# x and eps written into zeroed PSUM by ScalarE and VectorE instead of by identity matmuls, with x loaded one image of each half at a time

## The reference

```
x = x + L0(gn(x))    # contextual attention
x = x + L1(gn(x))    # 3x3 convolution, 64 to 64 channels, plus bias
```

## Time and profile before

| | us |
|---|---|
| median of 3 runs (lowest, highest) | 35.08 (35.05, 35.92) |
| the profiled execution | 34.43 |
| its span, first to last instruction | 32.5 |

### The profile page before, as it was taken

How to read it: one execution, slowest core, us unless ns; L and a number is a source line. 1 busy time by engine, 2 the same in 40 slices (tenths; PEclk the granted TensorE clock), 3 DMA queues, 4 the chain that set the end, 5 groups by cost and what they waited for, 6 DMA issues and landing times.

```text
span 32.5 us, 1877 instructions
## 1 busy us (share of the span) xinstructions
PE 26.9 (83%) x820; PEld 20.3 (62%) x820; DVE 17.8 (55%) x70; ACT 14.5 (45%) x41; POOL 12.6 (39%) x37
## 2 busy tenths in 40 slices
PE   0699999999969978995999799979999999991000
PEld 0314515317919957973998889749996999970000
DVE  0068280698479098459757183784869658005000
ACT  1940000697979992080934507078420890005000
POOL 3999999580676818870000000730028000000000
PEclk9999999999999999999999999999999999999999
DMA  0029679600000000000382000000000000440180
GB/s 0 0 55 303 174 215 365 234 0 0 0 20 0 0 0 0 20 0 10 49 113 35 5 0 0 20 0 0 0 20 0 0 0 20 163 160 0 39 284 0
DMA packets 4215, 1.87 MB, mean 58 GB/s; under 512 B 2800, under 2 KB 4080, under 8 KB 4208
## 3 DMA queue, kind: packets, MB, share of 16 engines
q1 hardware_dynamic: 3344, 1.24, 13.6%
q10 hardware_dynamic: 864, 0.53, 5.6%
HBM read 1.09 MB, written 0.52 MB: 50 GB/s over the span
## 4 chain that ended last, share of the span: by engine, by line
PE 66%; DVE 9%; POOL 9%; issue 5%; ACT 2%; POOLq 0%; DVEq 0%
PE X L508 20%; PE X L414 14%; PE X L486 13%; PE Y L498 4%; PE X L425 3%; PE Y L473 3%; DVE b_sb L672 3%; POOL rnorm L249 2%; ACT e_sb L339 2%; POOL gn_rstd L249 2%; PE X L418 2%; PE X L454 2%; PE X L444 2%; DVE pst L657 2%; DVE o_sb L704 1%
## 5 line engine op out<-in xcount | busy, mean ns | idle before, releaser
L414 PE MATMUL X<-idle 128*128 128x512 f16 x10 | 4.6, 607 | 1.1 <-POOL idle L230 1.1
L249 POOL TENSOR_TENSOR hn_rstd<-hn_mv,neg_half 128x2 f32<-128x2 f32 x2 | 1.4, 688 | 8.7 <-DVE hn_mv L602 8.7
L486 PE MATMUL X<-k_sb,pst 64*64 64x128 f32 (+2 forms) x144 | 4.4, 263 | 0.4 <-DVE pst L657 0.4
L508 PE MATMUL X<-x2h,whl 64*64 64x256 f16 x144 | 4.7, 274 | 0.0
L486 PEld LDWEIGHTS X<-k_sb,pst 64*64 64x64 f32 x144 | 3.9, 133 | 0.7 <-issue 0.5
L508 PEld LDWEIGHTS X<-x2h,whl 64*64 64x64 f16 x144 | 4.1, 106 | 0.0
L436 PE MATMUL X<-fst 64*64 64x64 f32 x144 | 2.7, 222 | 0.3 <-DVE fst L612 0.3
L414 PEld LDWEIGHTS X<-idle 128*128 128x128 f16 x10 | 1.0, 127 | 3.0 <-issue 1.9
L436 PEld LDWEIGHTS X<-fst 64*64 64x64 f32 x144 | 2.4, 134 | 0.7 <-DVE fst L612 0.7
L473 PE MATMUL Y<-xh,pair_k 64*64 64x256 f32 x16 | 2.8, 444 | 0.0
L508 PE MATMUL X<-x2l,whl 64*64 64x256 f16 x72 | 2.4, 274 | 0.0
(11 more groups left out here) (83 smaller groups left out, 56.9 us busy)
## 6 DMA issues: line engine op xcount, KB each, us to landing
k_sb<-k_dram SPq DMA_DIRECT2D x1, 288.0 KB, 3.6
xh<-x_in_dram SPq DMA_DIRECT2D x2, 128.0 KB, 3.0
xh<-x_in_dram ACTq DMA_DIRECT2D x2, 128.0 KB, 3.6
out_dram<-o_sb ACTq DMA_DIRECT2D x2, 128.0 KB, 2.1
out_dram<-o_sb SPq DMA_DIRECT2D x2, 128.0 KB, 2.1
k_sb<-c_dram SPq DMA_DIRECT2D x1, 192.0 KB, 3.3
whl<-whl SPq DMA_DIRECT2D x2, 72.0 KB, 3.1
w_sb<-weight_in_dram SPq DMA_DIRECT2D x1, 72.0 KB, 3.6
```

The source lines that it names most:

```text
L249: return pool.tensor_tensor(dst, src, neg_half[:, 0:dst.shape[1]], ALU.pow)
L414: te.matmul(fill_ps, idle[:, 0:P], idle[:, :], start=True, stop=True)
L486: i = te.matmul(b_ps[u][half(o ^ h), h, q0:q0 + step * (nq - 1) + 1:step, :], pst[u][half(o), 1 - t, h, G * (1 - s):G * (1 - s) + L], sh, ...
L508: i = te.matmul(conv_ps[u][half(t), h, :], whl[half(h), w, k, :], xp[u][half(h), t, k // 3:k // 3 + H, k % 3:k % 3 + W], start=False, stop ...
```

## The change

- x: the eight identity matmuls of `put_x` on PE are replaced by four ScalarE copies from SBUF to PSUM. For that each of the eight banks is first written once with zeros by one of the 512-column matmuls (`fill`), counted in `bank_set`; later matmuls in those banks add (`start=False`).
- eps: `add_eps` (eight matmuls before the first statistics, four at the end of each `deconv`) goes; VectorE writes eps into the zeroed banks after the third fill. `hn_ps[1]` moves from column 448 to 472. The fills in front of the first `pair_statistics` go from eight to seven; behind it one (the eighth bank) is added, and one more stands before `gram(0, 0)`.
- x loads: each is one image of each half, on 128 partitions, with a semaphore of its own, and the statistics of image t wait for load t alone. The output goes with it: a store now holds both images of one half (64 partitions), and waits for both ScalarE's and VectorE's result.
- zeroing: POOL zeroes only the borders of f, y, y1 and p, and the fp16 tensors as fp32 words; VectorE no longer zeroes f.
- lists: on PE the mask product goes between parts 0 and 1 of `gram(1)`, `transpose_f(1)` goes ahead of `fuse2(1)`, and `deconv(0)` has one shift of unit 1 ahead of it and three behind it, before the second statistics. On DVE `keep_mask` (now with a memset of `mask_ps` behind it) goes ahead of `normalise_gram(0)`, both `gated_weight` behind `largest(0)`, `copy_ft(1)` ahead of the wait for `deconv(0)`. On ACT the four `put_x` stand first, and `exp_logits(0)` ahead of `high_weight`.

```diff
-        fill_ps = X[0][:, 0, :]
-
-        xh_in = unit_sems("xh_in")
+        banks = [X[1][:, 1, :], X[1][:, 0, :], X[0][:, 0, :], Y[0][:, 0, :], Y[0][:, 1, :], Y[1][:, 0, :],
+                 X[0][:, 1, :], Y[1][:, 1, :]]
+
+        xh_in = [[sem(f"xh_in{u}{t}") for t in t2] for u in u2]
...
-        xhv = x.rearrange("(u h t) c s -> u h c t s", u=UNITS, h=2)
-        ov = out.rearrange("(u h t) c s -> u h (t c) s", u=UNITS, h=2)
...
+        xhv = x.rearrange("(u t h) c s -> u t (h c) s", u=UNITS, t=IPU)
+        ov = out.rearrange("(u t h) c s -> u t c h s", u=UNITS, t=IPU)
...
-            sp.dma_start(xh[0][half(0), :, :], xhv[0, 0]).then_inc(xh_in[0], 16)
-            sp.dma_start(xh[1][half(0), :, :], xhv[1, 0]).then_inc(xh_in[1], 16)
+            for u in u2:
+                sp.dma_start(xh[u][:, 0, :], xhv[u, 0]).then_inc(xh_in[u][0], 16)
...
-                sp.wait_ge(out_ready[u], 1)
-                sp.dma_start(ov[u, 1], o_sb[u][:, 1, :]).then_inc(stored, 16)
+                sp.wait_ge(out_ready[u], 2)
+                sp.dma_start(ov[u, 1], o_sb[u][half(1), :, :]).then_inc(stored, 16)
...
-            link(pool.memset(eps_sb[:, :, :], 0.0))
-            pool.memset(eps_sb[:, :, 2], GN_EPS * 2 * HW).then_inc(small_set, 1)
-            for u in u2:
-                pool.memset(y[u][:, :, :], 0.0).then_inc(att_zero, 1)
-                pool.memset(y1[u][:, :, :], 0.0).then_inc(att_zero, 1)
-            for u in u2:
-                pool.memset(pst[u][:], 0.0).then_inc(att_zero, 1)
-            for u in u2:
-                pool.memset(x2h[u][:, :, :, :], 0.0).then_inc(x2_zero, 1)
-                pool.memset(x2l[u][:, :, :, :], 0.0).then_inc(x2_zero, 1)
-            pool.wait_ge(small_set, 2)
+            for u in u2:
+                pool.memset(pads(fst[u][:]), 0.0).then_inc(f_zero, 1)
+                for edge in edges(fst[u]):
+                    pool.memset(edge, 0.0).then_inc(f_zero, 1)
+            for u in u2:
+                pool.memset(y[u][:, :, 0:PADL:PADL - 1], 0.0).then_inc(att_zero, 1)
+                pool.memset(y1[u][:, :, 0:PADL:PADL - 1], 0.0).then_inc(att_zero, 1)
+            for u in u2:
+                pool.memset(pads(pst[u][:]), 0.0).then_inc(att_zero, 1)
+                for edge in edges(pst[u]):
+                    pool.memset(edge, 0.0).then_inc(att_zero, 1)
+            for u in u2:
+                pool.memset(x2h[u][:, :, :, :].bitcast(fp32), 0.0).then_inc(x2_zero, 1)
+                pool.memset(x2l[u][:, :, :, :].bitcast(fp32), 0.0).then_inc(x2_zero, 1)
+            pool.wait_ge(small_set, 1)
...
-            act.dma_start(xh[0][half(1), :, :], xhv[0, 1]).then_inc(xh_in[0], 16)
-            act.dma_start(xh[1][half(1), :, :], xhv[1, 1]).then_inc(xh_in[1], 16)
+            for u in u2:
+                act.dma_start(xh[u][:, 1, :], xhv[u, 1]).then_inc(xh_in[u][1], 16)
...
+            def put_x(u, t):
+                act.wait_ge(bank_set, 1 + (3, 4, 5, 7)[2 * u + t])
+                act.wait_ge(xh_in[u][t], 16)
+                act.activation(x1_ps[u][:, t, :], xh[u][:, t, :], ACT.Copy).then_inc(x_put[u], 1)
...
-                act.activation(o_sb[u][:, 0, :], conv_ps[u][:, 0, :], ACT.Identity, bias=bias, scale=1.0 / W_SCALE).then_inc(act_step, 1)
-                act.wait_ge(act_step, u + 1)
-                act.dma_start(ov[u, 0], o_sb[u][:, 0, :]).then_inc(stored, 16)
...
+                act.activation(o_sb[u][:, 0, :], conv_ps[u][:, 0, :], ACT.Identity, bias=bias, scale=1.0 / W_SCALE
+                               ).then_inc(out_ready[u], 1)
+                act.wait_ge(out_ready[u], 2)
+                act.dma_start(ov[u, 0], o_sb[u][half(0), :, :]).then_inc(stored, 16)
...
+            for u in u2:
+                for t in t2:
+                    put_x(u, t)
             weight_scales()
...
+            exp_logits(0)
             high_weight()
-            exp_logits(0)
-            act.wait_ge(att_zero, 6)
+            act.wait_ge(att_zero, 10)
             left_of_p(0)
             copy_ft(0)
...
+            def fill(ps):
+                return te.matmul(ps, idle[:, 0:P], idle[:, :], start=True, stop=True)
+
             def keep_clock(n):
                 for _ in range(n):
-                    te.matmul(fill_ps, idle[:, 0:P], idle[:, :], start=True, stop=True)
-
-            def add_eps(ps):
-                for h in h2:
-                    te.matmul(ps[half(h), :, :], eye(h), eps_sb[half(h), :, :],
-                              start=True, stop=False, skip_group_check=True)
+                    fill(banks[6])
...
-                            i = te.matmul(gram_ps[u][half(t), h, :], f, f, start=n == di == 0, stop=n == 2 and di == 2)
+                            i = te.matmul(gram_ps[u][half(t), h, :], f, f, start=False, stop=n == 2 and di == 2,
+                                          skip_group_check=True)
...
-                te.wait_ge(x_put[u], 4)
+                if u:
+                    te.wait_ge(mask_gone, 1)
...
-            def put_x(u, t):
-                te.wait_ge(xh_in[u], 32)
-                for h in h2:
-                    te.matmul(x1_ps[u][half(h), t, :], eye(h), xh[u][half(h), t, :],
-                              start=True, stop=False, skip_group_check=True).then_inc(x_put[u], 1)
...
             def deconv(u):
                 te.wait_ge(ft_ready[u], 2)
                 te.wait_ge(b_ready[u], 2)
+                te.wait_ge(x_put[u], 2)
                 for q in range(4):
                     for h in h2:
                         for t in t2:
@@ -498,7 +513,6 @@
                             i = te.matmul(px[:, q // 2, q % 2], ft[u][half(t ^ h), h, q, :],
                                           b_sb[u][half(t ^ h), h, q, :], start=False, stop=True, skip_group_check=True)
                 i.then_inc(dec_done[u], 1)
-                add_eps(hn_ps[u])
...
             te.wait_ge(idle_set, 1)
-            keep_clock(4)
+            for ps in banks[0:7]:
+                fill(ps).then_inc(bank_set, 1)
             te.wait_ge(pair_k_set, 2)
-            te.wait_ge(small_set, 2)
-            add_eps(gn_ps[0])
-            add_eps(gn_ps[1])
-            keep_clock(4)
+            te.wait_ge(gn_eps, 1)
             pair_statistics(gn[0], gn_ps[0])
-            put_x(0, 0)
+            fill(banks[7]).then_inc(bank_set, 1)
             keep_clock(2)
             pair_statistics(gn[1], gn_ps[1])
+            keep_clock(1)
             gram(0, 0)
             gram(0, 1)
             gram(0, 2).then_inc(gram_done[0], 1)
-            put_x(0, 1)
             gram(1, 0)
+            te.wait_ge(k_late_in, 16)
+            te.wait_ge(mask_cell, 1)
+            te.wait_ge(bank_set, 8)
+            te.matmul(mask_ps, mint[:, :].broadcast_to([L, P]), kb(K_WINDOW)[half(0)], start=False, stop=True,
+                      skip_group_check=True).then_inc(mask_sum, 1)
             gram(1, 1)
             gram(1, 2).then_inc(gram_done[1], 1)
-            te.wait_ge(k_late_in, 16)
-            te.wait_ge(mask_cell, 1)
-            te.matmul(mask_ps, mint[:, :].broadcast_to([L, P]), kb(K_WINDOW)[half(0)], start=True, stop=True
-                      ).then_inc(mask_sum, 1)
             fuse1(0)
             transpose_f(0)
             te.wait_ge(mask_ready, 1)
             fuse2(0)
             fuse1(1)
-            put_x(1, 0)
-            put_x(1, 1)
+            transpose_f(1)
             fuse2(1)
             te.wait_ge(k_shift_in, 16)
             sum_shifts(0, range(9)).then_inc(b_done[0], 1)
-            transpose_f(1)
+            sum_shifts(1, range(0, 1))
             deconv(0)
-            sum_shifts(1, range(0, 3))
+            sum_shifts(1, range(1, 4))
+            te.wait_ge(hn_eps, 2)
             pair_statistics(hn[0], hn_ps[0])
-            sum_shifts(1, range(3, 9)).then_inc(b_done[1], 1)
+            sum_shifts(1, range(4, 9)).then_inc(b_done[1], 1)
             start_from_x1(0)
             deconv(1)
...
-            for u in u2:
-                dve.memset(fst[u][:], 0.0).then_inc(f_zero, 1)
-
-            def statistics(n, src):
+            dve.wait_ge(bank_set, 3)
+            eps_of_gn = X[1][:, :, 448:448 + 4 * STATS].rearrange("p h (t k) -> p h t k", t=2)[:, :, :, 2]
+            dve.memset(eps_of_gn, GN_EPS * 2 * HW).then_inc(gn_eps, 1)
+            for u in u2:
+                dve.memset(hn_ps[u][:, :, 2], GN_EPS * 2 * HW).then_inc(hn_eps, 1)
+
+            def statistics(n, src, landed=None):
                 for t in t2:
+                    if landed:
+                        dve.wait_ge(landed[t], 16)
                     dve.bn_stats(n.stats[:, t, :], src[:, t, :]).then_inc((n.half_stats, n.stats_ready)[t], 1)
...
+                dve.wait_ge(mask_ready, 1)
+                dve.memset(mask_ps, 0.0).then_inc(mask_gone, 1)
...
-            dve.wait_ge(xh_in[0], 32)
-            statistics(gn[0], xh[0])
+            statistics(gn[0], xh[0], xh_in[0])
             moments(gn[0], gn_ps[0])
```

(18 more changed lines are left out.)

21 lines of the change are left out of this document (12 added, 9 removed).

## The result

The changed kernel takes 36.4 us (median of five runs, 35.91 to 36.77) against 35.05 for the kernel before (34.05 to 35.92): a ratio of 1.058, 95% interval 1.039 to 1.076. It is slower. The prediction said 34.55, 34.0 to 35.35, with 6% for slower.

The account below looks back on a forecast made before the run. It took one chain of latencies, not one full engine, as the bound. Profiled 34.43 - 0.55 (convolution start) + 0.07 (stores) = 33.95; the median lies 0.65 above, 34.6; forecast 34.55 us, range 34.0 to 35.35.

Parts of the forecast that it names:

- GpSimd's border memsets replace larger ones; they end no later than before.: Front: GpSimd's zeroing was to end no later than before; no cost to VectorE was counted.
- done by 3.2: Front: VectorE's three eps memsets, behind the third fill at about 2.6, were to be done by 3.2 us.
- The pair statistics start at 4.7.: Front: first pair statistics on TensorE at 4.7 us against 5.28, a gain of 0.6.
- That rival: Front gains more: first load lands well before 4.0, everything before y(0) moves by -0.9; 34.0 to 34.3 us, chance 0.25.
- The clock.: Rival: gaps at 4.1 to 4.7 and around 6.5 delay TensorE's clock rise, y(0) at 12.1; 35.75 us, chance 0.08.
- The reciprocal behind turn_y1(1): Before the shifts: VectorE's gated weights delay turn_y1(1) to 14.3, reciprocal at 14.33 against 14.59; gain shrinks to 0.27 us.
- The convolution's 7.01 us stay.: End of the kernel: TensorE's convolution was to keep its length of 7.01 us, starting at 21.8 against 22.36.
- The tail, "+0.05": Stores by halves: bounds 0 and +1.5 us, +0.05 taken since KB and packet size are the same.
- The rival at +0.7 to +1.1: Very end: stores by halves land as the loads did, +0.7 to +1.1 us; 35.3 to 35.6, chance 0.08.
- put_x and ScalarE's copies: Taking put_x off TensorE is worth 0, as it lies in waits; ScalarE's copies take 375 ns each, with 0.3 us cover.
- y(0) starts directly behind keep_mask's memset: Before y(0): y(0) was to come at 11.0 us against 11.38, directly behind VectorE's memset ending at 10.98.
- The fills that "hold the chain up by 0.5 us": Front of the kernel before: four 512-column fills on TensorE delay the first pair statistics, ready at 4.78, by 0.5 us.

Follow-up runs that it names:

- pair_k_first: The changed kernel with GpSimd waiting for VectorE's pair_k before its border memsets; 35.59 us beside 35.10 for the kernel before, ratio 1.012.
- put_x_on_tensor: pair_k_first with put_x as identity matmuls on TensorE again, ScalarE's four copies gone; 35.18 us beside 34.25 for the kernel before, ratio 1.021.
- before_two_fills_less: The kernel before with two instead of four fills in the second keep_clock, nothing else; median 35.65 us beside 35.04.

## Why the prediction was wrong

- **"GpSimd's border memsets replace larger ones; they end no later than before."** This step failed. They do end earlier, at 3.9 instead of 5.8, but they start at 1.67, where the first eps memset stood (1.66), with no wait behind it, and hold VectorE's pair_k up until they are through: 2.50 us instead of 0.60. VectorE's eps memsets, put at "done by 3.2", began at 4.22. The prediction looked at when the memsets end and put their effect on VectorE at nothing. pair_k_first gives it 1.4 us at y(0), and in time about 4%, between ratios of 1.058 and 1.012 with wide intervals.
- **"The pair statistics start at 4.7."** 5.26, for that reason. The x loads were better than assumed: without the hold-up the statistics start at 3.15. That rival was right in its mechanism and gave 1.05 us at y(0) in pair_k_first; its chance of 0.25 was no use without the first step.
- **The clock.** The gap was foreseen as 4.1 to 4.7 and was 1.06 us. The rival was priced for a late rise; what came was an early rise and a fall, or a late rise in two kernels with the same front. y(0) at 11.8 to 12.5 in these three spans what it had worked out, 12.1. (Its sum adds 1.2 us for 12.1 in place of 11.0, which is 1.1.) So its direction was right and part of its reason: what brought the gap was the hold-up, which it did not have.
- **"The reciprocal behind turn_y1(1)"**, which made the weights shrink the gain from 0.4 to 0.27: it waited for exp in both orders. Their real price was on another engine: moving the weights moved GpSimd's low weights beside probabilities(0), 1.00 instead of 0.48 us. The prediction followed those weights only as far as SP's copies. This is the second failed step, of the same kind as the first.
- **"The convolution's 7.01 us stay."** 7.70 here (7.04 before, counted to the last result), 7.23 to 7.26 in the seven variants with the same ScalarE list ahead of the second x2h. 0.2 is ScalarE's late x2h, which comes and goes with the number of instructions ahead of it.
- **The tail, "+0.05".** +0.62. The bounds were right and the value taken was wrong: equal size and packets were taken for equal cost. The rival at +0.7 to +1.1 was nearer.
- **put_x and ScalarE's copies.** 378 ns a copy against the 375 forecast; that put_x off TensorE is worth nothing, as said, fits put_x_on_tensor, within its interval. y(0) starts directly behind keep_mask's memset (11.73, 0.11 us; y(0) at 11.76, the two overlapping by 0.09), as forecast.
- **The fills that "hold the chain up by 0.5 us".** Two of them less, in before_two_fills_less, gave 0.06 us at y(0), and the second norm came 0.67 us later behind deconv(0). In this kernel it is no safe step to take instructions away; the prediction had no term for it.

The pieces against the kernel before, in the two profiles: y(0) +0.38 (hold-up and clock, less what loads and fills gave), probabilities +0.52, convolution +0.67, tail +0.62, the rest +0.11; 2.3 us in all. Of the convolution's 0.67, 0.2 and more are shown as a pause that depends on place; the rest of the changed kernel's 7.70, with a stop of 0.26 at 28.85 (matmul 729), was seen once and stays open.

## What to carry to other kernels

When a list of small GpSimd instructions is moved or loses a wait, look at what VectorE runs beside it, and the other way round for VectorE instructions with two inputs: the price appears on the other engine, as a longer time of an instruction whose work has not changed (pair_k 2.50 instead of 0.60 us, the probabilities 1.00 instead of 0.48), and counts there as busy. A transfer's form (partitions and dimensions) has a price at either end of the kernel, so weigh the load that it shortens against the store that it lengthens. In a kernel of a few tens of microseconds, with hundreds of instructions a list, an ablation that takes instructions away also moves pauses, so read the trace for stops without a wait before the time is believed; met waits in their place are no sure remedy, as here they took one stop away and 0.41 us came elsewhere.

## What was not expected of the hardware

- A row of 20 GpSimd memsets, their starts 0.03 to 0.3 us apart, kept one VectorE tensor_scalar of 0.22 us going for 2.2 us, until the last was done.
- ScalarE started 0.35 us late, and TensorE's weight loads paused 0.3 to 1.06 us, with all waits met, at fixed places of their lists; met waits added ahead moved ScalarE's pause to another step. A packet for the engine's instructions follows 0.6 us behind ScalarE's pauses and 1.0 to 1.5 us behind TensorE's. Why TensorE stops in one kernel and not in the next stays open.
- Two stores of 64 partitions with two rows each took 0.67 us to issue instead of 0.36, and 2.7 instead of 2.1 to land; cut into four of one row each, the tail was as long (3.77 us).
